# Parts of q and k stored once in the scratch memory and read back in three runs

## The reference

```
q = (x @ wq.T).reshape(Bx, Tx, H, Dh).transpose(0, 2, 1, 3)
k = (x @ wk.T).reshape(Bx, Tx, H, Dh).transpose(0, 2, 1, 3)
v = (x @ wv.T).reshape(Bx, Tx, H, Dh).transpose(0, 2, 1, 3)
attn = jnp.einsum('bhqd,bhkd->bhqk', q, k) / scale
attn = attn + slopes[None, :, None, None] * dist[None, None, :, :]
attn = jax.nn.softmax(attn, axis=-1)
out = jnp.einsum('bhqk,bhkd->bhqd', attn, v)
out = out.transpose(0, 2, 1, 3).reshape(Bx, Tx, H * Dh)
x = _layernorm(x + out @ wo.T + bo)
```

## Time and profile before

| | |
|---|---|
| Median of 3 executions | 779.03 us |
| The profiled execution's own time | 778.99 us |
| Its span, first to last instruction | 777.0 us |
| PE busy | 744.8 us (96%) |
| DVE busy | 641.2 us (83%) |
| ACT busy | 598.6 us (77%) |
| POOL busy | 355.1 us (46%) |
| DMA, whole span | 88.72 MB, 177117 packets |
| HBM read, written | 49.39 MB, 37.22 MB |

### The profile page before, as it was taken

How to read it: one execution, slowest core, us unless ns; L and a number is a source line. 1 busy time by engine, 2 the same in 40 slices (tenths; PEclk the granted TensorE clock), 3 DMA queues, 4 the chain that set the end, 5 groups by cost and what they waited for, 6 DMA issues and landing times.

```text
span 777.0 us, 26998 instructions
## 1 busy us (share of the span) xinstructions
PE 744.8 (96%) x10262; PEld 542.4 (70%) x10262; DVE 641.2 (83%) x1316; ACT 598.6 (77%) x1083; POOL 355.1 (46%) x528
## 2 busy tenths in 40 slices
PE   5899999999999999999999999999999999999995
PEld 3566756676667676676765788887777777778874
DVE  4799989999899999998994767888777777777875
ACT  5588878788788888887888777777777777777773
POOL 5257969788576766666654301122221122221212
PEclk8699999999999999999999999999999999999998
DMA  5767767776656666666631112223222233332221
GB/s 159 181 175 163 192 161 195 177 189 175 158 156 150 171 172 166 168 149 166 156 102 51 36 33 48 61 54 68 57 57 59 56 68 68 68 68 65 59 54 57
DMA packets 177117, 88.72 MB, mean 114 GB/s; under 512 B 67760, under 2 KB 164080, under 8 KB 177008
## 3 DMA queue, kind: packets, MB, share of 16 engines
q1 hardware_dynamic: 174736, 83.60, 44.4%
q0 software_dynamic: 880, 2.88, 1.4%
q10 hardware_dynamic: 1392, 0.69, 0.3%
HBM read 49.39 MB, written 37.22 MB: 111 GB/s over the span
## 4 chain that ended last, share of the span: by engine, by line
PE 80%; DVE 5%; issue 4%; DMA 3%; SPq 3%; ACT 2%; POOL 1%; DVEq 0%; POOLq 0%; ACTq 0%
PE ps_o L583 17%; PE ps_b L1054 13%; PE ps_b L1057 13%; PE ps_a L505 12%; PE ps_b L513 6%; PE ps_b L640 3%; PE ps_b L601 3%; PE ps_a L520 2%; PE ps_a L1054 2%; PE ps_a L1057 2%; PE ps_a L623 2%; PE ps_a L609 2%; PE ps_b L520 2%; DVE gate_f L1274 2%; PE ps_b L631 1%
## 5 line engine op out<-in xcount | busy, mean ns | idle before, releaser
L829 DVE TENSOR_REDUCE neg_sb<-ps_a 128x2 f32<-128x512 f32 x512 | 322.0, 681 | 30.2 <-PE ps_a L520 23.8
L718 ACT ACTIVATE probs<-ps_b 128x512 f32<-128x512 f32 x512 | 275.7, 595 | 52.5 <-PE ps_b L520 36.7
L505 PE MATMUL ps_a<-qk_stack 52*64 52x256 bf16 x2048 | 174.8, 281 | 8.8 <-DMA qk_stack<-qk_scratch 6.6
L513 PE MATMUL ps_b<-qk_stack 54*64 54x256 bf16 x2048 | 168.5, 276 | 4.4 <-issue 2.9
L1168 ACT ACTIVATE gelu_f<-ps_b,sc 128x512 f32<-128x512 f32 x124 | 85.4, 689 | 77.0 <-PE ps_b L1057 76.3
L583 PE MATMUL ps_o<-probs,v_aug 128*32 128x256 f32 x2048 | 139.2, 387 | 2.7 <-issue 2.7
L505 PEld LDWEIGHTS ps_a<-qk_stack 52*64 52x64 bf16 x2048 | 83.7, 108 | 81.2 <-DVE neg_sb L829 40.6
L520 PE MATMUL ps_a<-corner_sb,eye_sb 64*64 64x128 bf16 x1024 | 116.7, 222 | 0.0
L520 PE MATMUL ps_b<-corner_sb,eye_sb 64*64 64x128 bf16 x1024 | 113.9, 218 | 0.0
L1054 PE MATMUL ps_b<-g2h,h_hi 128*128 128x512 f32 x256 | 102.2, 399 | 1.8 <-DVE gate_f L1274 1.6
L1054 PE MATMUL ps_b<-g1h,h_hi 128*128 128x512 f32 x256 | 101.3, 396 | 0.1
(11 more groups left out here) (129 smaller groups left out, 1497.4 us busy)
## 6 DMA issues: line engine op xcount, KB each, us to landing
qk_stack<-qk_scratch SPq DMA_DIRECT2D x126, 192.0 KB, 4.1
qk_scratch<-qk_sb SPq DMA_DIRECT2D x95, 128.0 KB, 2.2
qk_scratch<-qk_sb SPq DMA_DIRECT2D x63, 192.0 KB, 2.4
xT_sb<-in_xT SPq DMA_DIRECT2D x32, 128.0 KB, 4.5
x_sb<-in_x SPq DMA_DIRECT2D x32, 128.0 KB, 4.4
x_scratch<-x_sb SPq DMA_DIRECT2D x32, 128.0 KB, 4.3
x_res<-x_scratch SPq DMA_DIRECT2D x16, 256.0 KB, 2.8
out<-y_out SPq DMA_DIRECT2D x32, 128.0 KB, 1.9
```

The lines of the kernel that those rows point to most:

```text
L505: pe.matmul(ps[side * TILE:(side + 1) * TILE, qb * SEQ:(qb + 1) * SEQ], q_stack[i][rows_of, j, at:at + TILE], k_stack[i][rows_of, j, :], s ...
L513: pe.matmul(ps[side * TILE:(side + 1) * TILE, kb * SEQ:(kb + 1) * SEQ], k_stack[i][rows_of, j, at:at + TILE], q_stack[i][rows_of, j, :], s ...
L718: nc.scalar.activation(probs[:, h % HALF, :], ps_b[b_bank(t, k)][:], ACT.Exp, scale=slope[h]).then_inc(exp_done, 1)
L829: nc.vector.tensor_reduce(negmax[:, h_a // HALF, h_a % GROUPS, h_a % HALF // GROUPS, :], ps_a[a_bank(t, k)][:].rearrange("p (b k) -> p b k ...
```

## The change

Every part of q and k gets one place in scratch, and the terms arise when the places are read. There are ten places of 64 KB, of which six are written: q's hi, mid and lo in 0, 1 and 2, k's lo, mid and hi in 3, 4 and 5. Three writes of 128 KB, one after each splitting stage, replace five writes of 768 KB together. Three runs replace the two halves: run 0 reads places 0 to 2 for q and 3 to 5 for k (three terms, 24 partitions of each group), run 1 places 0 and 1, 4 and 5 (two terms, 16 partitions), run 2 places 0 and 5 (one term, 8 partitions). Each partition gets all eight heads of its group in one piece of 4 KB, where it got two pieces of 2 KB. The reads are still 768 KB for a sequence, in six DMAs of 192, 192, 128, 128, 64 and 64 KB. The terms are the same six, in another order of rows.

In the order of SyncE, runs 2 and 1 of a sequence stand right behind its spills, in front of the rows of the second maxima, and run 0 where all four reads stood, at the head of the next step. The reads wait for semaphores of their own for each of the three writes. PE waits at head 0 for all three runs, and no more at head 8. The first sequence keeps the old form, with a scratch tensor of its own.

```diff
-SPILLS = 5
+SPILLS_FIRST = 5
+SPILLS = 3
+RUNS = 3
+PLACES = 10
...
-            def spill(b, par):
-
-                parts, terms = qk_sb[par], qk_dram[par].rearrange("n r d h t -> n (d h) r t")
-                wait(sp, qk_first, b + 1)
+            def spill_first():
+
+                parts, terms = qk_sb[0], qk_first_dram.rearrange("n r d h t -> n (d h) r t")
+                sp.wait_ge(qk_first, 1)
                 sp.dma_start(terms[1, :, 0:3, :],
                              parts[:, 0, 1, :].unsqueeze(1).broadcast_to([P, 3, SEQ])).then_inc(spilled, DMA)
-                wait(sp, qk_second, b + 1)
+                sp.wait_ge(qk_second, 1)
                 sp.dma_start(terms[1, :, 3:5, :],
                              parts[:, 1, 1, :].unsqueeze(1).broadcast_to([P, 2, SEQ])).then_inc(spilled, DMA)
                 sp.dma_start(terms[0, :, 3:5, :], parts[:, 0:2, 0, :]).then_inc(spilled, DMA)
-                if b > 0:
-                    spill_last(sp, b, par)
-
-            def stack_part(b, pairs, signal):
-
-                src = qk_dram[b % 2].rearrange("n r d (g j) t -> g (r d) n j t", g=GROUPS)
+
+            def spill(b, par):
+
+                parts, places = qk_sb[par], qk_dram[par].rearrange("s d h t -> (d h) s t")
+                sp.wait_ge(qk_first, b + 1)
+                sp.dma_start(places[:, 0:6:5, :], parts[:, 0, :, :]).then_inc(hi_spilled, DMA)
+                sp.wait_ge(qk_second, b + 1)
+                sp.dma_start(places[:, 1:5:3, :], parts[:, 1, :, :]).then_inc(mid_spilled, DMA)
+                sp.wait_ge(qk_split, b + 1)
+                sp.dma_start(places[:, 2:4, :], parts[:, 2, :, :]).then_inc(lo_spilled, DMA)
+
+            def stack_first(pairs, signal):
+
+                src = qk_first_dram.rearrange("n r d (g j) t -> g (r d) n j t", g=GROUPS)
                 for g in range(GROUPS):
-                    dst = qk_stack[b % STACKS][g * TILE:g * TILE + STACK, :, pairs, :]
+                    dst = qk_stack[0][g * TILE:g * TILE + STACK, :, pairs, :]
                     sp.dma_start(dst.rearrange("p n j t -> p n (j t)"),
                                  src[g, :, :, pairs, :].rearrange("r n j t -> r n (j t)")).then_inc(signal, DMA)
 
-            def stack(b, half):
-
-                stack_part(b, slice(half * HH, (half + 1) * HH), stacked[b % 2][half])
+            def stack(b, run):
+
+                apart, count, row = ((3, 3, 0), (4, 2, 3 * DH), (5, 1, 5 * DH))[run]
+                src = qk_dram[b % 2][0:2 * apart].rearrange("(n s) d (g j) t -> g n s d (j t)", n=2, g=GROUPS)
+                for g in range(GROUPS):
+                    dst = qk_stack[b % STACKS][g * TILE + row:g * TILE + row + count * DH, :, :, :]
+                    sp.dma_start(dst.rearrange("p n j t -> p n (j t)"),
+                                 src[g, :, 0:count].rearrange("n s d c -> (s d) n c")).then_inc(stacked[b % 2], DMA)
...
                 if live(t + 2, BATCH) and t + 2 > 0:
-                    wait(sp, spilled, (t + 3) * SPILLS * DMA)
-                    wait(sp, scores_b, (t - 1) * HEADS)
-                    if t + 2 < STACKS:
-                        sp.wait_ge(rows_laid[t + 2], 2)
-                    for half in range(2):
-                        stack(t + 2, half)
+                    sp.wait_ge(lo_spilled, (t + 2) * DMA)
+                    stack(t + 2, 0)
...
                 if live(t + 3, BATCH):
-                    for half in range(2):
-                        wait(sp, stacked[1 - par][half], (t + 3) // 2 * GROUPS * DMA)
-                        if t + 3 == 2:
-                            sp.wait_ge(pair_landed[half], GROUPS * DMA)
-                    spill(t + 3, 1 - par)
+                    if t + 3 == 0:
+                        spill_first()
+                    else:
+                        wait(sp, stacked[1 - par], (t + 2) // 2 * RUNS * GROUPS * DMA)
+                        spill(t + 3, 1 - par)
+                if live(t + 3, BATCH) and t + 3 > 0:
+                    wait(sp, scores_b, t * HEADS)
+                    if t + 3 < STACKS:
+                        sp.wait_ge(rows_laid[t + 3], 2)
+                    sp.wait_ge(hi_spilled, (t + 3) * DMA)
+                    stack(t + 3, 2)
+                    sp.wait_ge(mid_spilled, (t + 3) * DMA)
+                    stack(t + 3, 1)
...
-                    if b_a == 0 and h_a in (0, GROUPS):
-                        pe.wait_ge(pair_landed[h_a // GROUPS], GROUPS * DMA)
-                    elif h_a == (2 * GROUPS if b_a == 0 else 0) or h_a == HALF:
-                        wait(pe, stacked[b_a % 2][h_a // HALF], (b_a // 2 + 1) * GROUPS * DMA)
+                    if b_a == 0 and h_a in (0, GROUPS, 2 * GROUPS, HALF):
+                        pe.wait_ge(first_landed[h_a // GROUPS if h_a < HALF else 3], GROUPS * DMA)
+                    elif b_a > 0 and h_a == 0:
+                        pe.wait_ge(stacked[b_a % 2], (b_a + 1) // 2 * RUNS * GROUPS * DMA)
...
-                wait(pool, spilled, (b - 1) * SPILLS * DMA)
+                if b == 2:
+                    pool.wait_ge(spilled, SPILLS_FIRST * DMA)
+                wait(pool, lo_spilled, (b - 2) * DMA)
+                wait(pool, mid_spilled, (b - 2) * DMA)
+                wait(pool, hi_spilled, (b - 2) * DMA)
...
-    qk_dram = nc.dram_tensor("qk_scratch", [2, 2, TERMS, DH, HEADS, SEQ], BF16, kind="Internal").ap()
+    qk_first_dram = nc.dram_tensor("qk_first_scratch", [2, TERMS, DH, HEADS, SEQ], BF16, kind="Internal").ap()
+    qk_dram = nc.dram_tensor("qk_scratch", [2, PLACES, DH, HEADS, SEQ], BF16, kind="Internal").ap()
```

25 lines of the change are left out of this document (12 added, 13 removed).

## The result

The changed kernel took 789.05 us (median of four executions, 786.15 to 791.12), the kernel before in the same runs 776.95 (four executions, 771.1 to 779.26). The ratio is 1.015, with a 95% interval of 1.010 to 1.020: slower by 1.5%, where 1.0% less was forecast, and outside the range. The profiled execution took 786.15 us, its span 784.2.

A forecast was written before the change was run, and what follows sets the result against it. PE bounds the kernel at 12.17 us a step, with 10.5 us lost to instruction transfers made late by spill bursts. 779.0 - 7.5 (writes) - 0.5 (start) = 771.0 us, other terms 0; range 763 to 780.

The forecast's parts named there:

- The steady pace: Attention steps: PE's own work takes 12.17 us a step and stays so, a change of 0.
- PE's late instructions: Attention: PE's unnamed stops read as instruction transfers made late by full DMA engines; 10.5 us lost together.
- The first rival: Attention: PE's stops stay, as traffic isn't their whole cause; only the start is left, 778.5 us; chance 0.25.
- The writes, -7.5: Spills of q and k: fewer bytes cut the time lost in PE's stops from 10.5 to 3.0 us.
- My own row against it: Between 251 and 253 us the DMA share is 1.10 and PE is busy all 2 us.
- The reads, 0: SyncE's six read issues for four: second maxima's rows at most 1 us later, needed 6 us on, so 0.
- PE's wait at head 0: 0: PE at head 0 needs all three runs; they land a half to 3 us early, so 0.
- The start, -0.5: PE's wait for sequence 1 at the start: ends -1.7 and +0.7 us, the middle -0.5 taken.
- the slower rival: Reads on fewer partitions land later and PE waits for them at head 0: 788 us; chance 0.10.
- The stops stay: The first rival by its title: PE's stops remain in the attention, giving 778.5 us; chance 0.25.
- The lower level: Whole kernel: most executions fall to the 771.1 us seen once in three, perhaps 763 with fewer stops; chance 0.12.

The follow-up runs named there:

- experiment 11: Changed kernel with GpSimd's split of a weight piece moved behind the second maxima, run again in more rounds: 771.19 us, 0.993 of the kernel before.
- experiment 5: Kernel before with half the writes (384 KB for 768 KB) in the same five issues, reads as before: 777.60 us, ratio 1.000.
- experiment 1: Changed kernel with the rows of the second maxima issued before runs 2 and 1, all six reads in one stretch: 795.69 us, 1.019 of the kernel before.
- experiment 3: Changed kernel with both the second maxima's rows issued before runs 2 and 1 and the weight piece split later: 789.62 us, 1.011 of the kernel before.
- experiment 2: Changed kernel with GpSimd's split of a weight piece moved behind the second maxima, q and k: 771.42 us, 0.989 of the kernel before.
- experiment 9: Changed kernel with each run read in two parts of four heads, 2 KB pieces, twelve issues for six: 782.40 us, 1.009 of the kernel before.
- experiment 10: Changed kernel with the weight piece split later and runs read in 2 KB pieces, twelve issues: 778.58 us, 1.003 of the kernel before.
- experiment 7: Kernel before, writes unchanged, with reads as runs of 24, 16 and 8 partitions all at the step's head: 833.67 us, ratio 1.069.
- experiment 4: Kernel before with GpSimd's split of a weight piece moved behind the second maxima: 776.91 us, ratio 0.996.
- experiment 6: Kernel before with two whole reads of 384 KB in 4 KB pieces for four of 192 KB, PE waiting at head 0: 810.44 us, ratio 1.045.

## Why the prediction was wrong

**The steady pace** was right: 12.17 us a step in every kernel wherever nothing is late.

**PE's late instructions** were read rightly, and the trace of before shows them in the queue q8, which brings packets of 16 KB. It has 61 packets from 60 to 400 us, one in 5.5 us in the median. That they are PE's is read from their times. The first line below is from that stretch; the second is from 90.3 to 99.4 us, ahead of the first stop of the earlier trace rows, and its two packets began at 90.36 and 99.33.

```profile
q8 instruction: 61, 1.00, 1.3%
...
q8 instruction: 2, 0.03, 2.0%
```

Before the four stops of the earlier trace rows the packets came 9.0, 7.4, 8.2 and 8.6 us after the one before. Each began 0.4 to 1.5 us ahead of the stop, so the stop is not what held it up, and PE went on 1.3 to 1.8 us behind its end. From 60 to 400 us every stop of more than 1 us inside a head, in any of the kernels here, comes behind a packet that followed 7.4 us or more after the one before, though two such gaps in the trace of before, of 7.4 and 7.5 us, cost less than half a microsecond; in experiment 11, where PE stops for no more than 0.7 us in these steps, no two packets are over 6.8 us apart. The two stops of the changed kernel at head 0 have it as well, 9.0 and 9.3 us. The first rival had this fetching hidden; at these stops it was not. What makes a packet late is another question.

**The writes, -7.5, is the first step that failed.** It took the late packets for a matter of the bytes in a step and read the price off two rows with different load. Half the writes alone gave back 1 us of 10.5 and no median (experiment 5). My own row against it, a full moment without a stop, was the better witness, and the first rival was right about the writes. Most of the stops of the earlier trace rows did go, and the second stretch did come down from 2.3 to 0.3 us, below what I had put there. What took them away is the way in which the reads are spread over the step: they are back in experiments 1 and 3, which have the new writes but all reads in one stretch, and they stay in 5, with old reads and few writes. How reads in one stretch make an instruction packet late I can't show.

**The reads, 0, is the second, and decided the sign.** Its sentence was that the rows of the second maxima go out "at most 1 us later" and are needed "half a step on, 6 us". In an undisturbed step that held: mostly 8.1 to 8.6 us behind the copy in experiment 2, 7.9 before. In the step shown with a weight piece they went out 2.0 later, and the slack from issue to need was 4.8 us, which their landing behind four reads used up and 1.57 more. I had followed what SyncE is moved past, but not what the slower reads do to a transfer of another queue: the piece, on which GpSimd waits in front of q and k. The row that could have warned was in the trace of before: GpSimd already waited 10.9 us for pieces, in eight of eleven steps, so there was no slack at that place, and most of what a piece lands later went on to the spill. Before, the rows had 6.8 us from issue to need in this step and 5.1 at least in the others, with no reads in front of them, and that covered the wait. Priced from there, 1.9 us of landing on each of eleven pieces can outweigh the 8 us that I had counted as gain. With GpSimd's order changed, the same change is worth 0.7% (experiment 11), which is near what I forecast, for another reason.

**PE's wait at head 0: 0** held: no stop there in 12 steps is put down to a run, and the two of 0.8 and 2.2 us have the late instruction packets named above. It holds because runs 2 and 1 go early; with all runs at the head it costs 1.2 to 2.5 us in a step with a weight piece (experiment 1).

**The start, -0.5,** measured +0.87. SyncE's rows, beside the earlier trace rows:

```profile
17.72 0.43 SPq L397 DMA_DIRECT2D qk_scratch<-qk_sb  x1
...
20.79 2.33 SPq L417 DMA_DIRECT2D qk_stack<-qk_scratch  x6
```

The reads begin at 20.79, not 19.8: 3.1 us after hi's issue, where I had a median landing of 2.2. They were all issued by 23.1, as worked out. But the last landed only when PE went on, at 28.65, 5.5 us later; I had 2.8 to 4.1 from reads of another form. This term is mis-sized by the landing, the same thing as in the slower rival. Experiments 9 and 10 keep it at 4.5 and 5.0 us with 2 KB pieces, so the size of a piece doesn't explain it.

**The rivals.** "The stops stay" was right that bytes are not the cause, wrong in 778.5. The slower one had a true mechanism, slow reads of few partitions (experiment 7), with 788 us close to the 789 measured, but that is a coincidence: what it named, head 0 waiting for runs, gave no stop that the profile names, and the loss came over the weight pieces to head 8. Its chance of 0.10 was too low, since I had let "landing today is never waited for" speak for a new form of read. The lower level of 771 us played no part: the changed kernel's four executions were all at 786 or more.

**Open.** What makes an instruction packet late. Why 4 KB pieces hold a DMA engine longer than two of 2 KB; what part of a run's late landing is its few partitions, its count of issues or its first place in the program. The Trainium skill's rule on how many engines a transfer uses, which the prediction cited, can't be read off any row: shares here are means over 16 engines.

## What to carry to other kernels

When a transfer gets another shape, ask who else uses the DMA engines, and look for the instruction that already waits for such a neighbour: it has no slack, and all that is queued behind it on its engine is late by the same time. Fewer bytes are worth nothing if no wait is made of bytes; test the term alone before building on it. A load that is needed much later than it is waited for should be consumed behind the work on the critical path: here this one move of two lines turned +1.5% into -0.7%.

## What the runs showed of the hardware

- 22 to 23 MB in 180 us held the DMA engines for 59.0% with reads in 4 KB pieces and 46.5% in 2 KB pieces (changed kernel, experiment 9), and a load of another queue landed 1.5 to 1.8 us sooner beside the 2 KB pieces, with GpSimd in either order (experiments 9 and 10). The piece alone does not set the landing (experiments 4 and 6: 5.2 us with 2 KB, 3.6 with 4 KB).
- In one step PE went on 6.9 us after the last issue of six reads of 24, 16 and 8 partitions in one stretch (experiment 1); four reads of 48 partitions land after 4.1 in the median.
- Two rows of 4 KB each, issued behind four such reads, were not there 4.8 us later, and PE's wait for them has no name in the profile. With no reads in front, 3.1 us were enough (experiment 5).
- A stop of PE with no releaser can be a late instruction packet: the stops of the earlier trace rows end 1.3 to 1.8 us behind the end of a 16 KB packet that came 7.4 to 9.0 us after the one before, where the median is 5.5.
